# Normalising the projected parameters inside the projection, and a new entry into the recurrence

## The reference

```python
xr, gate = jnp.split(x @ W_in.T, 2, axis=-1)
xr = xr + t_emb[:, None, :]
xc = silu(causal_conv4(xr) + b_conv)                       # 1024 channels
xn = (xc - mean(xc)) / jnp.sqrt(var(xc) + 1e-05) * ln_g + ln_b
Bm, Cm, dt = jnp.split(xn @ W_xproj.T, 3, axis=-1)         # 16 states each
dt = jnp.tanh(dt @ W_dt.T + b_dt) * 0.01
Ad = 1.0 + dt * -jnp.tanh(A_log)
Bd = Bm * jnp.minimum(jnp.linalg.norm(xn, axis=-1, keepdims=True), 1.0)
# over the tokens of a sequence, state h of 16 x 1024:
h = jnp.clip(h * ad[:, :, None] + bd[:, :, None] * xt[:, None, :], -10.0, 10.0)
yt = jnp.einsum('bd,bdh->bh', ct, h)
return (y + D * xn) * silu(gate) @ W_out.T
```

## Time and profile before

| | us |
|---|---|
| three runs, median (lowest to highest) | 3744.89 (3739.27 to 3748.81) |
| the profiled execution: time, span | 3736.37, 3734.6 |
| layer 0: projection, then recurrence | about 0 to 479, 479 to 1175 |
| attention layers | about 1175 to 2555 |
| layer 3: projection, then recurrence | about 2555 to 3039, 3039 to 3735 |
| busy over the span: PE, DVE, POOL, ACT | 91%, 80%, 50%, 36% |

### The profile page before, as it was taken

The page is one execution under the profiler, slowest core; times in us unless marked ns, Lnnn a source line. Parts: engine busy times, 40 slices in busy tenths (PEclk is TensorE's granted clock), DMA queues, the critical chain, the costliest instruction groups (busy, mean ns, idle before and its releaser), DMA issues. The chain is left out here.

```text
span 3734.6 us, 62216 instructions
## 1 busy us (share of the span) xinstructions
PE 3409.6 (91%) x22068; PEld 2261.9 (61%) x22068; DVE 2974.3 (80%) x3172; ACT 1354.1 (36%) x2078; POOL 1860.2 (50%) x1384
## 2 busy tenths in 40 slices
PE   8999949999996899999999999996999948999998
PEld 6777614444444667777777777775787733444444
DVE  4777879999995777777778777763576779999998
ACT  3555512122122454444444434432455532222221
POOL 2555756556553124444454444433355665556554
PEclk9999969999997899999999999998999979999999
DMA  4444465656653233222322222224344465665653
GB/s 129 154 176 180 187 217 207 219 204 209 217 204 126 81 101 120 77 85 84 106 94 93 76 82 85 73 64 130 119 180 170 170 232 194 220 208 204 220 206 136
DMA packets 257341, 563.90 MB, mean 151 GB/s; under 512 B 35008, under 2 KB 37440, under 8 KB 256992
## 3 DMA queue, kind: packets, MB, share of 16 engines
q1 hardware_dynamic: 252688, 553.63, 43.2%
q10 hardware_dynamic: 4384, 6.56, 0.5%
HBM read 390.75 MB, written 174.59 MB: 151 GB/s over the span
## 5 line engine op out<-in xcount | busy, mean ns | idle before, releaser
L1193 DVE CUSTOM_DVE_ANT_0 l0r_g<-l0r_g,l0r_pv,l0r_cf 128x1024 f32<-128x1024 f32 x512 | 641.8, 1336 | 9.0 <-PE l0r_pv L1002 7.4
L1193 DVE CUSTOM_DVE_ANT_0 l3r_g<-l3r_g,l3r_pv,l3r_cf 128x1024 f32<-128x1024 f32 x512 | 641.8, 1336 | 8.8 <-PE l3r_pv L1002 7.2
L137 PE MATMUL l1h_ps_p<-l1h_xh,l1c_wh 128*128 128x512 f32 x768 | 323.2, 421 | 5.7 <-issue 3.3
L139 PE MATMUL l1h_ps_p<-l1h_xl,l1c_wh 128*128 128x512 f32 x768 | 306.2, 399 | 0.0
L138 PE MATMUL l1h_ps_p<-l1h_xh,l1c_wl 128*128 128x512 f32 x768 | 304.9, 397 | 0.0
L2179 POOL TENSOR_TENSOR l1h_st<-l1h_veps 128x1 f32<-128x1 f32 x64 | 35.4, 553 | 534.3 <-DVE l1h_veps L2037 534.3
L1791 ACT ACTIVATE l1h_pt<-l1h_ps_t 128x512 f32<-128x512 f32 x256 | 151.2, 591 | 331.1 <-PE l1h_ps_t L1664 331.1
L1017 PE MATMUL l3r_py<-l3r_g,l3r_cd 128*32 128x512 f32 x2048 | 251.6, 610 | 0.0
L1017 PE MATMUL l0r_py<-l0r_g,l0r_cd 128*32 128x512 f32 x2048 | 251.6, 610 | 0.0
L2077 DVE TENSOR_TENSOR l1h_e<-l1h_e,l1h_mx 128x1024 f32<-128x1024 f32 x128 | 213.3, 1666 | 4.4
L2096 DVE TENSOR_TENSOR l1h_vt<-l1h_ps_p,l1c_dc 128x512 f32<-128x512 f32 x64 | 44.2, 691 | 192.8 <-PE l1h_ps_p L139 192.8
(11 more groups left out here) (400 smaller groups left out, 8961.8 us busy)
## 6 DMA issues: line engine op xcount, KB each, us to landing
l0r_x<-xhl_s SPq DMA_DIRECT2D x128, 512.0 KB, 5.7
l3r_x<-xhl_s SPq DMA_DIRECT2D x128, 512.0 KB, 5.6
xhl_s<-l0a_xo SPq DMA_DIRECT2D x58, 512.0 KB, 3.9
xhl_s<-l3a_xo SPq DMA_DIRECT2D x58, 512.0 KB, 3.9
gate_s<-l0a_gate SPq DMA_DIRECT2D x64, 256.0 KB, 2.4
l0r_dx<-dx_s SPq DMA_DIRECT2D x32, 512.0 KB, 7.4
l0r_gate<-gate_s SPq DMA_DIRECT2D x32, 512.0 KB, 8.4
l0r_crow<-feed_s SPq DMA_DIRECT2D x128, 128.0 KB, 2.9
```

The source lines that it names most:

```text
L137: pe.matmul(out, wh, xh, start=first, stop=False)
L139: return pe.matmul(out, wh, xl, start=False, stop=last)
L1193: dve._custom_dve(bass.dve_ops.TENSOR_ADD_SAT, out=g[:, t, j, :], in0=g[:, (t - 1) % TS, j, :], in1=pv[(k.off + t + j) % 3][:, :], s0=cf[: ...
```

## The change

`project_phase` normalises `proj` itself. VectorE gets `normalise(lo, hi)`, four chained products over 48 columns a sequence: at the end of step `it == 6` of tiles 2 to 6 for the four sequences of tile T - 2, after the last tile's taps for the next eight, and for the last four at the end. GpSimd gets the square roots in four pieces (`lengths`). After the last sequence VectorE, TensorE and ScalarE make decay, running products, reciprocal and feed, still in this phase; the last gates, halves and stores change their order, and SP takes two stores from ScalarE. In `recurrence_phase` only the feed's transposition and split are left ahead of block 0; block 0's weights no longer pass through DRAM: sixteen matmuls with selector matrices (made by GpSimd from `comb` and `ident`) spread the feed over partitions in PSUM, and VectorE masks it. ScalarE makes two of the three coefficient tables, GpSimd the third and the state's memset. The output weights are loaded in four loads of two into eight places (buffers that are free then), split by ScalarE after the first read-out copy and by GpSimd in two halves. Constants are loaded once, in the projection.

```diff
@@ project_phase @@
+        later_loads = [(same[:, :], cst["same"]), (ymask[:, :], cst["ymask"]), (comb[:, :], cst["comb"]),
+                       (alog[:, :], w["A_log"].rearrange("(a n b) -> a n b", a=1, b=1).to_broadcast([GB, NS, 1]))]
...
+            for dst, src in later_loads:
+                sp.dma_start(dst, src).then_inc(later, 16)
             for T in range(NT - 1):
...
+            store_split(B - 1, 1)
+            store_skip(B - 1)
...
-                if c == 6:
+                if c == 5:
                     xproj_turn(T)
+            for c, col in enumerate((2, 0)):
+                pe.wait_ge(ready, c + 1)
+                for j in range(GJ):
+                    last = pe.transpose(ptr[:, c * TW + j * S:c * TW + (j + 1) * S], proj[:, col, GB * j:GB * (j + 1), :].rearrange("p b n -> p (b n)"), ident[:, :])
+                last.then_inc(swung, 1)
...
+            act.wait_ge(later, 16 * len(later_loads))
+            act.activation(acol[:, 0:1], alog[:, :], ACT.Tanh).then_inc(tanh, 1)
+            act.wait_ge(swung, 1)
+            act.activation(decay.rearrange("p j s -> p (j s)"), ptr[:, 0:TW], ACT.Tanh).then_inc(tanh, 1)
...
+            def normalise(lo, hi):
+                dve.wait_ge(proj_ev, hi // TB)
+                dve.wait_ge(bn, 3 * hi)
+                dve.wait_ge(rstd, hi)
...
+                chain(dve.tensor_tensor(m, mean, total, ALU.mult))
+                chain(dve.tensor_tensor(rows_p, rows_p, m, ALU.subtract))
+                chain(dve.tensor_tensor(rows_p, rows_p, factor, ALU.mult))
+                return dve.tensor_tensor(rows_p, rows_p, offset, ALU.add)
...
                     add_taps(T, it)
                     if TB <= it < KI - 1:
                         split_low(T + 1, it - TB)
+                    if it == KI - 2 and T > 1:
+                        chain(normalise(TB * (T - 2), TB * (T - 1)))
...
                 add_taps(NT - 1, it)
+            chain(normalise(B - TB - GB, B - TB))
             for b in range(TB):
                 centre(B - TB + b)
                 rescale_shift(B - TB + b)
+            keep_projection(NT - 1)
+            normalise(B - TB, B).then_inc(ready, 1)
...
+            dve.wait_ge(root, 4)
+            chain(dve.tensor_scalar(norm[:, :], norm[:, :], 1.0, None, ALU.min))
+            dve.wait_ge(ready, 1)
+            dve.tensor_tensor(proj[:, 0, :, :], proj[:, 0, :, :], norm[:, :].unsqueeze(2).to_broadcast([P, B, NS]), ALU.mult).then_inc(ready, 1)
...
+            for j in range(GJ):
+                chain(dve.tensor_tensor_scan(prod[:, j, :], decay[:, j, :], zero, 1.0, ALU.mult, ALU.add))
+            inv = proj[:, 2, :, :]
+            chain(dve.reciprocal(inv, prod.rearrange("p j (a b) -> p (j a) b", b=NS)))
+            dve.wait_ge(swung, 2)
+            chain(dve.tensor_tensor(feed.rearrange("p j (a b) -> p (j a) b", b=NS), ptr[:, TW:2 * TW].rearrange("p (a b) -> p a b", b=NS),
+                                    inv, ALU.mult))
...
+            def lengths(lo, hi):
+                pool.wait_ge(ss, hi)
+                pool.wait_ge(halved, 2)
+                pool.tensor_tensor(norm[:, lo:hi], stat[:, lo:hi, 3], half[:, :].to_broadcast([P, hi - lo]), ALU.pow).then_inc(root, 1)
...
+                if n in (2 * GB + TB, 3 * GB + 2, B - TB):
+                    lengths(*{2 * GB + TB: (0, 2 * GB), 3 * GB + 2: (2 * GB, 3 * GB), B - TB: (3 * GB, B - TB)}[n])
+            lengths(B - TB, B)
@@ recurrence_phase @@
-                        load_x(1, 1)
-                        load_tokens(0, 0)
                         store_feed()
-                        load_feed(0, 0)
                         load_feed(1, 1)
+                        load_x(1, 1)
+                        load_tokens(0, 0)
...
-                        for c in range(KI):
-                            at_least(sp, w_lo, c - 1)
-                            sp.dma_start(wst[:, c % 2, :], w_out[:, c, :]).then_inc(w_ld[c % 2], 16)
+                        for m in range(KI // 2):
+                            sp.dma_start(stages[m], w_out[:, 2 * m:2 * m + 2, :]).then_inc(w_ld[m], 16)
...
+            for c in range(2):
+                pool.tensor_tensor(picks[c], comb[:, :].unsqueeze(1).to_broadcast([32, PAIR, PICK]),
+                                   ident[0:32, PAIR * c:PAIR * c + PAIR].unsqueeze(2).to_broadcast([32, PAIR, PICK]), ALU.mult).then_inc(pick, 1)
...
+            pool.memset(g[:, TS - 1, :, :], 0.0).then_inc(gup, GJ)
...
+            for c, half in enumerate((feed_h, feed_l)):
+                pe.wait_ge((feed_high, feed_low)[c], 1)
+                for t in range(TS):
+                    for e in range(2):
+                        last = pe.matmul(pv[2][:, t * 2 * P:(t + 1) * 2 * P],
...
+            for c in range(PAIR):
+                dve.wait_ge(picked, c + 1)
+                dve.tensor_tensor(wv[:, 0, TS * c:TS * (c + 1), :], pv[2][:, 512 * c:512 * (c + 1)].rearrange("p (a i) -> p a i", a=TS),
+                                  same[:, :].unsqueeze(1).to_broadcast([P, TS, P]), ALU.mult).then_inc(first_w, 1)
```

More of the change, by code:

```diff
@@ L188, in project_phase @@
         raw = ph.sb("raw", [P, TW])
-        bst = ph.sb("bst", [P, 2, 6])
-        veps = ph.sb("veps", [P, 2])
+        bst, veps = ones[:, HALF_P:HALF_P + 12].rearrange("p (a c) -> p a c", a=2), ones[:, HALF_P + 12:HALF_P + 14]
         mhalf = ph.sb("mhalf", [P, 1])
+        norm, half, acol = ones[:, 0:B], ones[:, B:B + 1], ones[:, B + 1:B + 3]
+        spent = xc[:, 0, :, :].rearrange("p k n -> p (k n)")
+        decay = spent[:, 0:TW].rearrange("p (j s) -> p j s", j=GJ)
+        zero = spent[:, TW:TW + S]
+        feed, prod = (carry[:, c * TW:(c + 1) * TW].rearrange("p (j s) -> p j s", j=GJ) for c in range(2))
         pxr = [ph.ps(f"pxr{k}") for k in range(2)]
@@ L202, in project_phase @@
             "loaded", "folded", "copied", "scaled", "summed", "kept"))
+        step, ready, swung, tanh, root, later = (ph.sem(n) for n in ("step", "ready", "swung", "tanh", "root", "later"))
         zeroed, halved, paired = ph.sem("zeroed"), ph.sem("halved"), ph.sem("paired")
@@ L574, in _ @@
             for c in range(KI):
+                if c in (3, 4, 6, 7):
+                    n = B - TB + (3, 4, 6, 7).index(c)
+                    halves(n)
+                    store_high(n)
                 silu_gate(T, c)
@@ L794, in recurrence_phase @@
         pzo = ph.ps("pzo")
[L795 to L801, removed]
@@ L819, in recurrence_phase @@
         block = ph.block()
+        stages = (dx[:, 1, :, :], gate[:, 1, :, :], wst[:, :, :], xr[:, :, :])
         n_pairs = NBLK // 2
@@ L962, in body @@
                         bounds(k + 1, 1 - q)
[L963 to L968, removed]
+                        weigh(k + 1, 1 - q, i + 1)
                     if not (first and q == 0):
@@ L972, in body @@
                         readers(k + 1, 1 - q)
+                    if first and q == 1:
+                        low_weights(KI // 2, KI)
                     if not first:
@@ L978, in body @@
                     gating(k, q, 0, i + 1)
+                    if first and q == 0:
+                        low_weights(0, KI // 2)
             blocks(pool, n_pairs, body)
@@ L984, in _ @@
         def _(pe):
[L985 to L991, removed]
             for j in range(GJ):
@@ L994, in _ @@
             last.then_inc(feed_turned, 1)
+            for j in range(GJ):
+                last = pe.transpose(pc[:, j * S:(j + 1) * S], proj[:, 1, GB * j:GB * (j + 1), :].rearrange("p b n -> p (b n)"), ident[:, :])
+            last.then_inc(read_turned, 1)
+            pe.wait_ge(pick, 2)
+            for c, half in enumerate((feed_h, feed_l)):
[3 more added lines that the diff above has]
+                        last = pe.matmul(pv[2][:, t * 2 * P:(t + 1) * 2 * P],
+                                         picks[t // PAIR][:, t % PAIR, HALF_P - 32 * e - c:HALF_P - 32 * e - c + P],
+                                         half[0:32, 2 * e:2 * e + 2, :], start=c == e == t % 2 == 0, stop=c == e == t % 2 == 1)
+                    if c == 1 and t % PAIR == 1:
+                        last.then_inc(picked, 1)
             def spread(k, t, p):
@@ L1118, in body @@
                     k = 2 * i + q
-                    if first and q == 0:
-                        for c in range(KI):
-                            act.wait_ge(w_ld[c % 2], 16 * (c // 2 + 1))
-                            act.activation(woh[:, c, :], wst[:, c % 2, :], ACT.Copy).then_inc(w_hi, 1)
                     if not (first and q == 0):
@@ L1130, in body @@
                     keep_y(k, 0)
+                    if first and q == 0:
+                        for c in range(KI):
+                            act.wait_ge(w_ld[c // 2], 16)
+                            act.activation(woh[:, c, :], stages[c // 2][:, c % 2, :], ACT.Copy).then_inc(w_hi, 1)
             blocks(act, n_pairs, body)
```

178 lines of the change are left out of this document (85 added, 93 removed).

## The result

| us | before | after |
|---|---|---|
| median of four runs (lowest to highest) | 3743.61 (3739.27 to 3748.81) | 3772.23 (3765.01 to 3775.75) |
| the profiled execution, its span | 3736.37, 3734.6 | 3765.01, 3763.2 |

The ratio is 1.0073, with a 95% interval of 1.0054 to 1.0093: slower by 28.6 us. The forecast was 3774. The profiled execution, 3765.01, stands beside a sum of 3765.4.

A forecast was written before the change was run, and what follows sets the result against it. TensorE was taken to bound the projection loop, one cross-engine chain the entry to the recurrence. Loop losses 38 + 21 less entry gain 30 gave +29 on the profiled 3736.4, 3765.4, hence a median of 3774; range 3718 to 3790.

The forecast's parts named there:

- The loop, layer 0: Normalisation in layer 0's projection loop: two products wait for GpSimd, 7.7 us lost per tile, five tiles 38 us, bounds 7 to 40.
- the clock's share: TensorE at half clock after its pause in the loop: 1.8 us a tile in layer 0, half of 0 to 1.8 in layer 3.
- the faster rival: In the loop, 192-column products slip past GpSimd: layer 0 loses 7, layer 3 nothing; -23, 3722 us; chance 0.22.
- The loop, layer 3: Normalisation in layer 3's projection loop: third and fourth products held, `evacuate` 4.3 us late; five tiles 21 us, bounds 0 to 26.
- The entry: From projection's end to first scan: the shortened chain gains 15 us a layer, 30 in all, bounds 20 to 38.
- The minimum: In the entry, after GpSimd's last product: the minimum's start was taken as 480.5, with ends 478 and 483.
- the phase change: Entry, between the feed being ready and the recurrence phase: at most 2.0 us, from 488.1 to 490.1.
- the last arm: Longest of three paths from phase change to first scan (weights 6.3, GpSimd 7.2, x 6.8): 7.2 us.
- GpSimd's arm: Entry, after the phase change: two selector products of at most 1.27, the state's memset 3.7, then 1.04; 7.2 us.
- At nothing: Tail normalisation, first roots, constants' loads and output weights were counted as covered, output weights with about 2 us to spare.
- VectorE keeping its turn: In the loop, VectorE waits for GpSimd's shift once only: layer 0 loses 27, layer 3 nothing; -3, 3742 us; chance 0.14.
- A late entry: At the entry, x or the memset comes 5 us later: +10 on the forecast, 3784 us; chance 0.12.

The follow-up runs named there:

- the five experiments: Normalisation at step 1, second inputs in PSUM, four products in the kernel before, two of four products, no normalisation in the loop: 3710.48, 3726.46, 3795.34, 3743.92, 3735.64 us.
- the last experiment: Changed kernel without normalisation in the loop, its twenty sequences done in the tail instead: 3735.64 us beside 3740.26 for the kernel before, ratio 0.9984.

## Why the prediction was right

**The loop, layer 0** (38 predicted, 38.7 measured). The step on which all hung, that GpSimd comes in between two chained products, held to 0.2 us: first and second held, last two free, `evacuate` 5.79 late instead of 5.9. TensorE's wait grew by 5.7 a tile; the other 2.1 of the 7.7, the clock's share, are near the 1.8 taken from the earlier trace rows. A nearer row than the attention's stood in this very loop. In step 5 of tiles 1 to 6 of the kernel before, `split_low`, also with two SBUF inputs, takes 2.69 or 2.70 instead of 0.68, because GpSimd's low half holds it. Timeline of before, tile 4:

```profile
280.52 2.40 POOL L749 TENSOR_TENSOR l0a_xo<-l0a_xn,l0a_xo 128x1024 fp32r<-128x1024 f32 x1 [1.00 <-ACT l0a_xo L522]
...
280.78 2.70 DVE L601 TENSOR_TENSOR l0a_xl<-l0a_xt,l0a_xh 128x512 fp32r<-128x512 f32 x1
```

With this row less could be said for the faster rival.

**The loop, layer 3** (21 predicted, 19.4 measured). The order was as forecast, third and fourth product held; `evacuate` was 4.2 late (4.3), TensorE's wait 2.94 instead of 3.4. Halving the clock's share was a bet between two ends, and that the mean bears it out is luck: the clock fell behind two of the five pauses, the first and the last, and not at all behind three. Table by stage of after, behind the first pause of the layer and in and behind the third; both pauses last 2.94:

```profile
2770.00:2772.00 2.00, 2.00 (x5) 1.54 (x6) 1.65 (x5) 1.89 (x3) 0.34 (x1) 0.50 0.37 132
...
2884.00:2886.00 2.00, 0.00 (x0) 0.00 (x0) 0.69 (x1) 1.27 (x3) 0.00 (x0) 1.00 0.00 0
2886.00:2888.00 2.00, 1.20 (x5) 1.03 (x6) 1.89 (x3) 2.00 (x5) 0.00 (x0) 1.00 0.00 0
```

The five tiles cost 4.6, 3.2, 3.2, 3.2 and 5.4; 3.9 in the mean, of which 0.95 are over the wait.

**The entry** (15 a layer predicted, 17.1 and 17.7 measured). Counted from the end of GpSimd's last product, 20.4 were predicted and 18.0 measured. The minimum started 2.05 after it instead of 3.6; the feed took 7.70 instead of 7.6; the phase change 1.55 instead of at most 2.0; the last arm 6.7 instead of 7.2. The mis-sized terms are the minimum's start and GpSimd's arm. For the selectors the bound of 1.27 was taken, and they took 0.82 each, so GpSimd was done 5.0 after the phase change and the weights came last, at 6.7 (6.3 predicted; their matmuls took about 1 more than taken). The two held products of the last normalisation (2.12 and 2.38 above) were foreseen.

**At nothing.** In layer 0 the output weights had no 2 us to spare: the first mix came 39.6 after the first scan, TensorE waiting 0.68 for GpSimd's half. In layer 3 it came at 38.3, without a wait. Layer 0's recurrence as a whole is 0.8 longer, so this costs under 1 there.

**What the sum left out.** The attention, which the change doesn't touch, takes 1373.2 from VectorE's first instruction there to its first in layer 3, and 1378.8 after. That isn't the change: in the five experiments it took 1380.6, 1377.9, 1371.6, 1374.9 and 1381.0, and the shortest of these is the kernel before with four products added. The work there is the same each time. The granted clock goes with it: in the stretches from the shortest to the longest it stood at 0.50 for 75, 76 (before), 78, 81, 85 (after), 90 and 91 us. What lets it fall more in one execution than in another isn't shown. These 9 us are as large as the spread between runs of one kernel, and the 5.5 stand against the entry's extra gain (two layers by 2 to 3) in this sum, so that the total agrees better than its terms by luck.

**The rivals.** Products that slip past GpSimd fell in the first row of the loop (2.55 for 0.36). VectorE keeping its turn fell in the second (2.38). A late entry didn't happen.

**The rule.** The Trainium skill (SBUF — State Buffer, Who interferes with whom) has the pairs right: two SBUF inputs held, one SBUF input not, here shown by one kernel with the input in PSUM. GpSimd's root fell the other way again: in the tail of after one over 8 columns ran from 482.00 to 483.96, and VectorE's products of two SBUF inputs at 482.49 and 483.08 took their undisturbed 0.56. To go by the row there was right for VectorE's products. The root itself looks held: one of VectorE's products with two SBUF inputs was under way when it started, until 482.45, and it ended 1.51 after that. In the last experiment it ran from 444.46 to 446.22, and VectorE's product under way ended at 444.71: 1.51 again.

## What to carry to other kernels

A chain of short VectorE products with two SBUF inputs is priced by the GpSimd products that run at that moment, one product held by each, and not by its columns; put it where one GpSimd product at most is under way and where the next thing VectorE owes the busiest engine isn't due. One line that moved the chain by a few steps turned 0.7% slower into 0.7% faster. Ask of every instruction put into a loop what stands behind it on its engine and how much slack that has; in layer 0 TensorE already waited 0.33 us there, so it had none to give. And look in the loop itself for an instruction that is held already: its row prices the next one.

## What the runs showed of the hardware that was not expected

Pauses of TensorE of one length, 2.94 us in layer 3 and 2.75 in the kernel with PSUM inputs, are followed by a granted clock of 0.50 in some tiles (two of five, three of five) and 1.00 in the others. All five pauses of 6.0 were followed by 0.50 and by a longer tile than the wait explains. What decides between them wasn't tried. A power on GpSimd took 2.93 us for 16 columns and 1.00 to 1.13 for 4; of the 1.96 and 1.76 for 8, 0.46 and 0.26 lie ahead of the end of VectorE's product, and of the 6.91 for 32, 1.62 lie ahead of the end of VectorE's first product. Without these parts it is 0.17 a column for 32, 0.18 for 16, 0.19 for 8 and 0.25 for 4, as an estimate: cheaper per column on many columns than on few.
